# Four-step sums for the denominators in the first three quarters of turns 9 and 12 of an attention kernel's score loop

## What is computed

```python
def _L0_xattn_ref(x1, x2, wq, wk, wv, wo, bo):
    b, n, _ = x1.shape
    m = x2.shape[1]
    q = (x1 @ wq.T).reshape(b, n, HEADS, HEAD_DIM).transpose(0, 2, 1, 3)
    k = (x2 @ wk.T).reshape(b, m, HEADS, HEAD_DIM).transpose(0, 2, 1, 3)
    v = (x2 @ wv.T).reshape(b, m, HEADS, HEAD_DIM).transpose(0, 2, 1, 3)
    dots = jnp.einsum('bhnd,bhmd->bhnm', q, k) * SCALE
    attn = jax.nn.softmax(dots, axis=-1)
    out = jnp.einsum('bhnm,bhmd->bhnd', attn, v)
    out = out.transpose(0, 2, 1, 3).reshape(b, n, DIM)
    return out @ wo.T + bo
```

## Time and profile before

| | us |
|---|---|
| three runs: median (lowest to highest) | 1892.88 (1891.89 to 1894.24) |
| span of the profiled execution | 1892.5 |
| score loop, exponentials of turns 0 to 15 | 475 to 1390 |
| turn 5 (all four quarters as sums of four) | 51.4 |
| turn 9 | 58.7 |
| turn 12 | 58.4 |

### The profile page before, as it was taken

How to read it: one execution, slowest core, us unless ns; L and a number is a source line. 1 busy time by engine, 2 the same in 40 slices (tenths; PEclk the granted TensorE clock), 3 DMA queues, 4 the chain that set the end, 5 groups by cost and what they waited for, 6 DMA issues and landing times.

```text
span 1892.5 us, 26855 instructions
## 1 busy us (share of the span) xinstructions
PE 1871.9 (99%) x10104; PEld 1284.5 (68%) x10104; DVE 1248.8 (66%) x2354; ACT 892.8 (47%) x1603; POOL 824.0 (44%) x745
## 2 busy tenths in 40 slices
PE   9999999999999999999999999999999999999998
PEld 8886787788555555555445545544459998899986
DVE  6675574278677788888778778778664444444447
ACT  4312323221665666666456456646734433344333
POOL 4002201100687888888667657656012123222232
PEclk9999999999999999999999999999999999999999
DMA  8003535684767585757644525442234454444544
GB/s 285 23 1 117 174 110 174 199 245 142 164 140 163 112 197 129 165 113 160 139 116 106 135 51 145 113 96 78 85 117 144 136 137 114 118 105 130 149 104 158
DMA packets 124498, 250.13 MB, mean 132 GB/s; under 512 B 11312, under 2 KB 29504, under 8 KB 119680
## 3 DMA queue, kind: packets, MB, share of 16 engines
q1 hardware_dynamic: 109696, 187.56, 33.6%
q0 software_dynamic: 14672, 60.85, 15.8%
HBM read 148.46 MB, written 62.42 MB: 111 GB/s over the span
## 4 chain that ended last, share of the span: by engine, by line
PE 84%; DVE 11%; DMA 2%; issue 1%; POOL 1%; ACT 0%; SPq 0%; DVEq 0%; ACTq 0%; POOLq 0%
PE banks L1211 36%; PE banks L1519 12%; PE banks L1406 11%; PE banks L1376 11%; PE banks L1395 9%; DVE max L1734 8%; PE banks L1427 4%; PE banks L1217 2%; DMA raw<-in_x_t 1%; DVE den_c L1753 1%; DMA k_half<-in_xwk_t 0%; PE banks L1307 0%; POOL x_nat L2261 0%; PE banks L1384 0%; DMA x_rows<-x_nat 0%
## 5 line engine op out<-in xcount | busy, mean ns | idle before, releaser
L1734 DVE TENSOR_REDUCE max<-banks 128x1 f32<-128x512 f32 x1024 | 626.9, 680 | 128.6 <-PE banks L1376 127.8
L2250 POOL TENSOR_TENSOR probs<-probs,probs 128x512 f32<-128x512 f32 x464 | 583.0, 1293 | 233.3 <-PE banks L1406 233.3
L2122 ACT ACTIVATE probs<-banks 128x512 f32<-128x512 f32 x1024 | 521.2, 607 | 260.7 <-PE banks L1395 259.9
L1376 PE MATMUL banks<-k_stack,q_stack 98*128 98x512 f32 x1024 | 427.5, 425 | 0.0
L1395 PE MATMUL banks<-q_stack,k_stack 98*128 98x512 f32 x1024 | 375.6, 397 | 2.1 <-ACT probs L2122 2.1
L1376 PEld LDWEIGHTS banks<-k_stack,q_stack 98*128 98x128 f32 x1024 | 191.5, 187 | 191.7 <-DVE max L1734 108.4
L1406 PE MATMUL banks<-probs,v_grp 128*32 128x512 f32 x2048 | 250.6, 602 | 0.0
L1395 PEld LDWEIGHTS banks<-q_stack,k_stack 98*128 98x128 f32 x1024 | 191.6, 188 | 58.3 <-ACT probs L2122 13.8
L2297 POOL DMA_INDIRECT y_rows<-eo,tok x35 | 69.7, 1993 | 170.8 <-DVE eo L1949 117.2
L1936 DVE TENSOR_TENSOR hid_lo<-hid,hid_hi 128x640 fp32r<-128x640 f32 x64 | 52.7, 824 | 126.4 <-ACT hid_hi L2197 126.4
L1406 PEld LDWEIGHTS banks<-probs,v_grp 128*32 128x32 f32 x2048 | 60.0, 109 | 108.5 <-issue 102.3
(11 more groups left out here) (269 smaller groups left out, 2817.9 us busy)
## 6 DMA issues: line engine op xcount, KB each, us to landing
k_stack<-k_parts SPq DMA_DIRECT2D x144, 256.0 KB, 5.3
probs<-probs POOLq DMA_DIRECT2D x36, 1024.0 KB, 9.9
w_raw<-in_L_ffn_w SPq DMA_DIRECT2D x16, 2048.0 KB, 9.4
q_stack<-q_parts SPq DMA_DIRECT2D x48, 256.0 KB
v_grp<-v_rows SPq DMA_DIRECT2D x48, 256.0 KB, 3.4
raw<-in_ctx_t SPq DMA_DIRECT2D x8, 1024.0 KB, 6.5
k_parts<-out_hi SPq DMA_DIRECT2D x32, 256.0 KB, 2.5
k_parts<-out_lo SPq DMA_DIRECT2D x32, 256.0 KB, 3.0
```

The costliest lines, as they stand in the source:

```text
L1376: nc.tensor.matmul(out, queries_of(t)[:, j, tile_of(k)], keys_of(t)[0:STK + SHIFT, j, mc * HALF:(mc + 1) * HALF], start=True, stop=True) \
L1734: V.reduce_max(max4[:, tiles_of(t), :, :][:, k, j, mc:mc + 1], bank(bank_of["max", t, mc, k, j]), AX.X) \
L2122: S.activation(probs_of(t, s)[:, j, :], bank(bank_of["score", t, s, j]), ACT.Exp, scale=SCALE) \
L2250: G.tensor_tensor(a[:, j, :], a[:, j, :], b[:, j, :], ALU.add).then_inc(pair_added.sem, 1)
```

## The change

Six more quarters are summed by fours: the first three of turns 9 and 12. The third quarter of each of these turns enters `LAST_BEFORE_PLAIN`, because the fourth quarter of the turn stays with sums of two. Nothing else is edited; what follows from the two sets is written out by the planner.

```diff
-LAST_BEFORE_PLAIN = {(2 * NG - 1, 2)}
+LAST_BEFORE_PLAIN = {(2 * NG - 1, 2), (9, 2), (12, 2)}
 
-LATER_FOURS = {(8, 0), (8, 1), (10, 1), (13, 0), (13, 1)}
+LATER_FOURS = {(8, 0), (8, 1), (9, 0), (9, 1), (9, 2), (10, 1), (12, 0), (12, 1), (12, 2), (13, 0), (13, 1)}
```

## The result

The changed kernel takes 1900.82 us, median of 6 runs (1898.60 to 1901.22), against 1893.59 for the kernel before in 6 runs on the same chip (1891.89 to 1894.24). The ratio is 1.0033, 95% interval 1.0022 to 1.0043: slower by 0.33%, 7.2 us. The forecast was 1893.6, within 1890.0 to 1896.4. The profiled span grew from 1892.5 to 1899.2, by 6.7 us.

The account below looks back on a forecast made before the run. PE and DVE both stood near their limits, decided block by block. Turn 12 at +0.8 us and turn 9 at -0.1 made +0.7, added to the median 1892.9: 1893.6 us, range 1890.0 to 1896.4.

Parts of the forecast that it names:

- The price of a tile and DVE's cover: Turns 9 and 12: tile removed 0.85 us, doubled 0.86; removal pays only where DVE waited for PE; sum +0.7 us.
- (A): Turns 9 and 12: PE alone sets the pace, three banks absorb DVE's lag; -5.1 us, 1887.8; chance 0.09.
- (B): Turns 9 and 12: DVE's cover is wider, no removed tile pays, four doubled ones cost 3.4 us; 1896.3; chance 0.09.
- (C): Turns 9 and 12: PE's earlier start lets DVE take up more than counted, half of (A); 1890.3; chance 0.06.
- (E): Turns 9 and 12: DVE binds throughout, by the skill's rule; 0 us, 1892.9; chance 0.71 together with the forecast.
- Block 9.3: Turn 9, block 9.3: its removed tile gains 0.0 us, since the next block lies inside DVE's packed stretch.
- The landings: Third quarters' transfers, tiles of 10.0 and 13.0: landing after 9.9 us leaves 6.0 to spare, 1.7 at the longest, 14.2.
- (D): Ends of turns 9 and 12: third quarter's transfer lands late, past 15.9 us, and PE waits; 1899.0; chance 0.05.
- The other queues: POOL, SP, DMA and PE's new wait: six more POOL issues of 0.87 us each, end cost 0 to 0.6 us.
- the cost on the end is 0, and up to 0.1 us an issue, 0.6 in all, if that cover were gone: POOL's queue, turns 9 and 12: the issues' delay of additions behind them is hidden, or nearly so.
- I give contention nothing: DMA engines, turns 9 and 12: shares 0.46 and 0.44 lie below turn 5's 0.67, so 0 us.
- the cover: POOL ahead of most blocks' additions: it waits for PE's numerators anyway, 1.76 us before those of 9.5.

Follow-up runs that it names:

- the two-transfer kernel: Kernel before with sums of four added only in the third quarters of turns 10 and 12: 1891.22 us, ratio 0.9983 to the kernel before.
- the CAST inside the run: Changed kernel with two reductions put ahead of the index search, so the CAST comes during POOL's second addition behind the issue: 1897.06 us, one run.
- the two with small additions: Changed kernel with three small POOL additions: in the issue's old place, issue moved behind the four additions, 1896.23 us; between issue and additions, 1899.88 us.

## Why the prediction was wrong, point by point

**The price of a tile and DVE's cover: right.** A removed tile was 0.85 in 9.1, 9.4 and 12.6, a doubled one 0.86 in 10.0, 12.7 and 13.0; 12.1 to 12.3 gave nothing for theirs; 12.4 gave 0.07 for 0.1. 9.6 and 9.7 together made +0.83 where -0.1 + 0.86 were forecast. In turn 12 the steps made +0.8, as the forecast had it. Rivals (A), (B), (C) and (E) are refuted by the same lines: tiles in 12.6 and 9.4 paid in full, those in 12.1 to 12.3 didn't.

**Block 9.3: off, behind the failure.** Forecast 0, measured -0.81. This block lies right behind the standstill: while PE still ran at the lower clock, DVE was no longer the one that others waited for. In the kernel with the issue behind the additions the same block gave -0.19. Without the first quarter's transfer the same block, with its tile removed, shows 0.0, as forecast; and in the kernel before with a later CAST it shows -0.18 with no tile removed. So the tile isn't what pays there, and I count it to the standstill's account, 6.43 - 0.81 = 5.6 us net. How the standstill does it is argued, not shown.

**The landings: right.** The six new transfers landed 9.9 to 12.9 us after their issue, and no matmul of L1427 waited for one. The two third quarters landed at 1035.4 and 1224.0, and their tiles, the first of the two in 10.0 and 13.0, began at 1039.79 and 1228.51: 4.4 and 4.5 us to spare, against 6.0 in the sum. All transfers of the line, after, against 6.9/9.9/14.2 in the earlier trace rows:

```profile
DMA to landing us min/median/max: 6.9/10.4/14.2
```

(D) stayed out in the changed kernel. Its mechanism is real, as the two-transfer kernel shows, but there it decided from a landing of about 13.7 us (14.79 - 1.07) and not of 15.9: the removed tiles of 12.5 and 12.6 bring PE 1.73 us sooner to the tile it waits for.

**The other queues: the step that failed.** It was the sentence "the cost on the end is 0, and up to 0.1 us an issue, 0.6 in all, if that cover were gone", and the "I give contention nothing" beside it. It counted an issue as 0.87 us of POOL's queue and asked only what stands behind it on that queue. Both halves missed.

First, the cover was read at one block (1.76 us before 9.5's additions) for all six issues, while at 9.2 it was 1.36 us, and the same change shrank it: PE's numerators come 0.85 us sooner with the tile of 9.1 gone, and an issue of 0.83 comes in front. 1.36 - 0.85 - 0.83 is below nothing. What the removed tile pays for PE, it takes from POOL's idle time.

Second, and this is the price, POOL's work has a victim on another engine. I priced the issue by who stands behind it on POOL, and never asked which instruction of DVE runs beside the additions that it moves. The short CAST, in none of my rows, stands ahead of a reduction that frees a bank. The term put at 0 to 0.6 us measured 6.43 in block 9.2: 4.9 more for the CAST (5.11 - 0.18) and 0.85 more for L1834 (1.34 - 0.49) on DVE, and on PE, for which that was a gap of 5.34, another 2.0 at the lower clock. Without that one transfer 9.0 to 14.0 took 5.4 us less (317.63 against 323.04), with the CAST out of its way 4.8 less. "I give contention nothing" had looked at the DMA engines' share only.

**Was it to be seen before?** The long wait was not: the three issues of before that stand directly ahead of additions stretch them, but have none of DVE's small instructions beside them. The short wait was. From the timelines of the kernel before, DVE and POOL, early in turn 14:

```profile
1317.55 1.21 DVE L1865 TENSOR_TENSOR col_s<-weight 128x4 f32<-128x4 f32 x1
1318.79 1.22 DVE L1866 TENSOR_SCALAR col_s<-col_s 128x4 f32<-128x4 f32 x1
```

```profile
1316.21 5.01 POOL L2250 TENSOR_TENSOR probs<-probs,probs 128x512 f32<-128x512 f32 x4 [2.49 <-PE banks L1406]
```

Four numbers per partition in 1.2 us is no cost of the work; each lasts to the end of an addition of POOL, the second (1318.76) and the third (1320.01) of the four. A rival "DVE's small instructions of 9.2 fall into the additions" at one addition, 1.2 us or a little over, could have been written from these rows; with the issue placed behind, it measured +3.59 in the block, since the clock fell as well. At 1.2 us such a rival would have stood at about 1895, inside the range; only with the 3.6 that was measured later does it come to about 1897, beyond the range and still short of 1900.8.

**What the skill says to it.** The Trainium skill (SBUF — State Buffer, Who interferes with whom) says that VectorE and GpSimd share one port pair under an exclusive lock, which a VectorE instruction needs when it has two SBUF inputs or runs in a two-port mode, as a cast can, and that whichever of the two issued first holds the other out for its whole instruction. The waits that end with the running addition, 1.18, 0.60 and 0.62 us, agree with it, and so do two of the three of block 8.7. The 5.11 us don't: behind an issue the wait goes over four instructions of POOL (3.69 us when it starts in the second). Nor do the 1.34 and 1.97 us of L1834, which with no issue ahead go past the end of an addition to that of the divide, or of the small additions behind it. So here the measurement decides.

**What stays open.** Why an issue directly ahead changes the additions behind it: the runs show that it does, that it is gone once POOL has idled, and that neither the moment of DVE's instruction nor which of the two forms it has matters, but no mechanism. Idle time and delay were not told apart: in all fourteen profiles POOL's work behind an issue is stretched where it begins 0.7 us or less behind the issue's start, and the additions are ordinary where they begin 1.1 us or more behind it, and nothing lies between. Three of the experiments (the CAST inside the run and the two with small additions) rest on one execution each. With the CAST moved away, PE stands idle for only 0.19 and 0.69 us of 9.2's 8.81, and of the 2.0 us left above its own 5.96 at most 1.7 can be the lower clock's (3.4 us at half pace); what the block would take without L1834's wait was not tried. Nor was it tried whether another transfer of the same length issued from another queue would do the same.

## What to carry to other kernels

Before an instruction is put ahead of others on POOL, list DVE's small instructions that run beside it, and ask of each whether it ends with an instruction of POOL: where one already does, price every further meeting at up to a whole POOL instruction, 1.2 us here, and behind a transfer's issue at the whole unbroken run of them, 5.1 us here. Two rows show where that can be: an instruction of DVE that is long for its size, and additions on POOL that take 5.15 us or more instead of 5.02 behind an issue. Idle time of an engine is a cover only at the block where it was read and only until the change moves the engine that ends it; here the gain itself (0.85 us sooner on PE) used it up. And a stall of PE is charged twice where the granted clock falls behind it, as in the 5.34 + 2.0 us of block 9.2.

## What the runs showed of the hardware

- Additions of 128x512 on POOL last 1.27 to 1.29 us and overlap by 0.04; directly behind the issue of an accumulating transfer, 1.5 to 1.6 us with 0.3 to 0.4 of overlap, four in 5.12 to 5.37 instead of 4.96 to 5.04; small ones 0.5 instead of 0.27. A CAST of 0.18 us on DVE that meets such a run waits to its end: 5.11, 5.13, 5.73 and, entered late, 3.69 us; written with two sources, 5.13. Row maxima beside such a run are not lengthened: 8 in 4.87 us.
- Small POOL instructions directly behind one another can hold DVE as well, even without an issue ahead: L1834 took 1.35 us through the end of an addition and the divide, and 1.97 us through the end of an addition, the divide and three additions of 0.27.
- With PE idle for 5.34 us in a block, but also for 1.40 and 0.69, the granted clock spent 6.8 us at its lower level, with score products 0.43 us apart instead of 0.23; with the CAST moved away, PE idle for 0.19 and 0.69, it was 3.4 us. Two kernels whose block 9.2 was as long as that one's, +1.87 and +1.92, kept the full clock, the second with PE idle for 1.48 and 0.69, so the length of PE's waits alone doesn't tell it. In blocks 2.2 and 2.3 it fell while PE was busy 7.9 of 8 us, for 6.8, 3.4 or 0 us from one profiled execution to another.
- One of the accumulating transfers took 14.8 us to land where their median is 10.3, and that was one that PE waited for.
